# A four-block transformer kernel on one core: the first attention's start reordered, its weight rounding moved to ScalarE and VectorE, and 18 weight-chunk sums moved to VectorE

## The reference, cut to what matters

```python
x = x + attn0(layernorm(x), Wqkv, bqkv, Wo, bo)      # x: 1024 rows of 512
x = x + ffn0(layernorm(x), w1, m1, w2, m2, w3, m3)
x = x + attn1(layernorm(x), ...)                      # 32 heads, top-128 index mask
x = x + lora_ffn(layernorm(x), ...)

def attn0(x, Wqkv, bqkv, Wo, bo):                     # one head of width 128
    q, k, v = split(x @ Wqkv + bqkv)
    return softmax(q @ k.T / sqrt(128)) @ v @ Wo + bo

def ffn0(h, w1, m1, w2, m2, w3, m3):                  # inner width 1792
    W = m + mean(abs(w - m)) * sign(w - m)            # for each of the three pairs
    return (silu(h @ W1.T) * (h @ W3.T)) @ W2.T
```

## Time and profile before

| what | value |
|---|---|
| median of 3 runs | 1438.15 us (1436.08 to 1439.1) |
| time of the profiled execution | 1438.22 us |
| its span, first to last instruction | 1436.4 us |
| mean granted TensorE clock | 0.967 of full speed |
| busy share of the span | PE 92%, PEld 76%, DVE 76%, ACT 58%, POOL 46% |
| matmuls | 7147 |

### The profile page before, as it was taken

How to read it: one execution, slowest core, us unless ns; L and a number is a source line. 1 busy time by engine, 2 the same in 40 slices (tenths; PEclk the granted TensorE clock), 3 DMA queues, 4 the chain that set the end, 5 groups by cost and what they waited for, 6 DMA issues and landing times.

```text
span 1436.4 us, 21267 instructions
## 1 busy us (share of the span) xinstructions
PE 1316.1 (92%) x7147; PEld 1096.2 (76%) x7147; DVE 1091.6 (76%) x2226; ACT 833.0 (58%) x1819; POOL 660.9 (46%) x651
## 2 busy tenths in 40 slices
PE   2968999999899789998769999999999999999998
PEld 1756888888789677775457888888888888888876
DVE  6357334343647599999979998898989889888976
ACT  3783532233246566774557767666776776667761
POOL 5460210010037445645656556555665565566534
PEclk9978999999999899998679999999999999999999
DMA  6560310000212333654720000000000000000021
GB/s 212 159 186 1 117 37 1 1 20 0 69 39 67 107 91 117 227 177 147 276 93 14 1 29 28 28 29 28 19 10 28 28 29 28 29 28 1 16 81 59
DMA packets 83706, 95.52 MB, mean 67 GB/s; under 512 B 11792, under 2 KB 59280, under 8 KB 83088
## 3 DMA queue, kind: packets, MB, share of 16 engines
q1 hardware_dynamic: 83600, 94.17, 20.9%
HBM read 75.27 MB, written 18.87 MB: 66 GB/s over the span
## 4 chain that ended last, share of the span: by engine, by line
PE 68%; DVE 17%; ACT 5%; issue 3%; DMA 2%; SPq 1%; POOL 1%; ACTq 0%; DVEq 0%
PE ps L350 16%; PE ps L352 15%; PE ps L351 15%; PE ps L1877 9%; PE ps L1897 3%; PE ps L1896 3%; DVE acc L1398 3%; DVE top L1409 2%; DVE xn_l L1471 1%; DVE rop L1421 1%; DVE acc L1412 1%; DVE rop L1419 1%; DVE pm L1451 1%; DMA iwq_raw<-in_L_attn_idx_wq_w 1%; DVE rop L1420 1%
## 5 line engine op out<-in xcount | busy, mean ns | idle before, releaser
L753 POOL TENSOR_SCALAR pm<-pm,smx 128x128 f32<-128x128 f32 (+1 forms) x255 | 189.4, 751 | 207.7 <-DVE smx L1458 207.7
L1055 ACT ACTIVATE pm<-pm,smx 128x128 f32<-128x128 f32 (+7 forms) x256 | 197.3, 772 | 35.3 <-DVE smx L1451 34.4
L1451 DVE CUSTOM_DVE_ANT_0 pm<-ps,mbias 128x128 f32<-128x128 f32 (+7 forms) x256 | 191.5, 752 | 27.4 <-PE ps L1877 13.1
L1877 PE MATMUL ps<-ident,pm 128*128 128x128 f32 x1152 | 175.0, 276 | 7.3 <-DVE pTa_l L1471 2.0
L1061 ACT ACTIVATE xn_h<-ps 128x512 fp32r<-128x512 f32 (+3 forms) x256 | 128.6, 513 | 84.1 <-PE ps L1877 81.3
L1471 DVE TENSOR_TENSOR xn_l<-ps,xn_h 128x512 fp32r<-128x512 f32 (+3 forms) x256 | 144.5, 587 | 24.8 <-ACT xn_h L1061 23.8
L350 PE MATMUL ps<-latT_l,qc_h 128*128 128x512 f32 (+3 forms) x384 | 143.3, 373 | 16.7 <-DVE smx L1451 8.7
L1877 PEld LDWEIGHTS ps<-ident,pm 128*128 128x128 f32 x1152 | 132.3, 141 | 33.9 <-issue 11.3
L352 PE MATMUL ps<-latT_h,qc_h 128*128 128x512 f32 (+3 forms) x384 | 134.1, 349 | 0.0
L351 PE MATMUL ps<-latT_h,qc_l 128*128 128x512 f32 (+3 forms) x384 | 133.6, 348 | 0.0
L1398 DVE SCALAR_TENSOR_TENSOR acc<-ps,iw,acc 128x768 f32<-128x768 f32 (+4 forms) x105 | 87.2, 877 | 25.1 <-ACT ps L941 24.6
(11 more groups left out here) (294 smaller groups left out, 3717.8 us busy)
## 6 DMA issues: line engine op xcount, KB each, us to landing
iwq_raw<-in_L_attn_idx_wq_w SPq DMA_DIRECT2D x48, 256.0 KB, 3.5
base<-in_L_ffn_mean_w SPq DMA_DIRECT2D x28, 256.0 KB, 3.1
wring<-in_L_ffn_w SPq DMA_DIRECT2D x21, 256.0 KB, 3.8
ow_raw<-in_L_attn_o_w SPq DMA_DIRECT2D x8, 512.0 KB, 3.9
xn_t<-in_L_attn_o_w SPq DMA_DIRECT2D x8, 512.0 KB, 4.2
wuvo<-pr_even SPq DMA_DIRECT2D x8, 512.0 KB, 5.1
wuvo<-pr_hl SPq DMA_DIRECT2D x8, 512.0 KB, 4.7
wuvo_h<-wuvo SPq DMA_DIRECT2D x16, 256.0 KB, 2.6
```

Of the source, the lines that this page charges most:

```text
L753: pool.tensor_scalar(pm[:, i % 4, 0:w], pm[:, i % 4, 0:w], smx[:, 32 + i:33 + i], 0.0, ALU.mult, ALU.add).then_inc(hd_p, 1)
L1055: act.activation(pm[:, i % 4, 0:w], pm[:, i % 4, 0:w], ACT.Exp, bias=smx[:, i:i + 1], scale=-1.0, accum_out=smx[:, 16 + i:17 + i]).then_in ...
L1451: dve.tensor_tensor_reduce(out=pm[:, i % 4, 0:w], in0=two_banks(2 * (i % 2), w), in1=mbias[:, TRI[t]:TRI[t + 1]], scale=1.0, scalar=3.0 * BIG,
L1877: done = pe.transpose(ps[:, t_bank(p, i), tile(k)], pm[:, tq % 4, tile(4 * c + k)], ident[:])
```

## The change

- Each score row of tile 4 starts at column 192 of the pair of banks, so that it is a matmul of 320 columns in either bank (`row_parts`, `row_block`). The number of matmuls is the same.
- Wqkv is rounded by one ACT instruction and its remainder taken by two DVE instructions (`wqkv_h`, `wqkv_l`), in the first half of the norm; POOL no longer does it. ACT waits for the four loads on `ld_a` ahead of its first `norm_hi`.
- PE makes q of the first four tiles before it transposes tile 4, and a quarter of k of the first four tiles after each of the tiles 4 to 7. Then a value tile, then q and k of the other four. The transposes of this norm use banks 4 and 5.
- Of 18 chunks (kind G) ACT does the sign alone, with no drain, and DVE takes the sum of absolute values from the ring slot. The slot's next load waits for both (`wt_sum`). The others (kind C) stay as they were.
- The bias row is added tile by tile ahead of chunks 16, 18, 20, 22 and 28 (tiles 4 to 7). The first load of w2 waits for all eight.
- The next norm's first `half_norm` and ACT's square root table stand ahead of T7 (N0). The matmul that adds the sums stands behind T7 (M0) and waits for the sums of both engines.

```diff
-ATT_PE = items("S0 S1 V0 V1 V2 V3 Z0 S2 V4 V5 V6 V7 T0 S3 T1 S4 T2 S5 T3 S6 O0 T4 S7 Y0 Y1 T5 Y2 T6 Y3 T7 O1 "
+ATT_PE = items("V1 S0 S1 V2 V3 S2 Z0 V4 V5 V6 V7 T0 S3 T1 S4 T2 S5 T3 S6 O0 T4 S7 Y0 Y1 T5 Y2 T6 Y3 T7 M0 O1 "
                "Y4 Y5 Y6 Y7")
-ATT_ACT = items("C1 S0 S1 C2 V0 C1 S2 C2 V1 T0 C1 T1 S3 C1 T2 S4 C1 T3 S5 C2 S6 C2 O0 T4 C1 S7 C1 T5 C2 T6 C2 T7 O1")
-ATT_DVE = items("S0 S1 V0 B0 S2 V1 T0 S3 T1 S4 T2 S5 T3 S6 O0 T4 S7 Y0 Y1 T5 Y2 T6 Y3 T7 O1 Y4 Y5 Y6 Y7")
-FIRST_CHUNKS = {3: 4, 7: 2}
-ADD_AT = {16: 0, 20: 4}
+ATT_ACT = items("G1 S0 G1 S1 G2 V0 G2 S2 G2 V1 T0 G1 T1 S3 C1 G1 T2 S4 C1 G1 T3 S5 C1 G1 S6 C1 G1 O0 T4 G1 S7 C1 T5 G2 "
+                "T6 N0 T7 O1")
+ATT_DVE = items("S0 S1 A2 V0 A2 S2 B0 A2 V1 A2 T0 S3 A1 T1 S4 A1 T2 S5 A1 T3 S6 A1 O0 A1 T4 S7 A1 Y0 Y1 T5 Y2 A2 T6 Y3 "
+                "N0 T7 O1 Y4 Y5 Y6 Y7")
+FIRST_CHUNKS = "CCCGGCC"
+ADD_AT = {16: (0,), 18: (1,), 20: (2,), 22: (3,), 28: (4, 5, 6, 7)}
...
+ROW_AT = {4: 192}
...
+        def row_parts(b, t):
+            w, at = (t + 1) * P, ROW_AT.get(t, 0)
+            cut = min(512, at + w)
+            parts = [(slice(0, cut - at), ps[:, b, at:cut])]
+            if at + w > 512:
+                parts.append((slice(cut - at, w), ps[:, b + 1, 0:at + w - 512]))
+            return parts
...
                 if last is not None:
                     sp.wait_ge(wt_abs, last + 1)
+                    if last in SUM_APART:
+                        sp.wait_ge(wt_sum, SUM_APART.index(last) + 1)
...
+                if CHUNK_KIND[chunk] == "G":
+                    act.activation(sgn[m][:, s * width:(s + 1) * width], slot, ACT.Sign).then_inc(wt_abs, 1)
+                else:
...
+            first_sqrt(0)
+            act.wait_ge(ld_a, 64)
+            act.activation(wqkv_h[:], raw[:], COPY).then_inc(at_wh, 1)
+            for t in range(4):
+                norm_hi(0, t)
+            weight_chunk()
+            weight_chunk()
+            first_sqrt(1)
+            weight_chunk()
+            for t in range(4, NT):
+                norm_hi(0, t)
+                if t < 6:
                     weight_chunk()
+            first_evict(0)
+            first_evict(1)
+            weight_chunk()
+            first_evict(2)
+            weight_chunk()
+            first_evict(3)
...
+            def first_weights(half):
+                k = slice(2 * half, 2 * half + 2)
+                dve.wait_ge(at_wh, 1)
+                dve.tensor_tensor(wqkv_l[:, k, :], raw[:, k, :], f(wqkv_h[:, k, :]), ALU.subtract).then_inc(at_w, 1)
...
+            def chunk_sum():
+                chunk = apart.pop(0)
+                dve.wait_ge(wt_d, chunk + 1)
+                dve.tensor_reduce(absum[:, chunk:chunk + 1], ring(chunk), AXX, ALU.add, apply_absolute_value=True)\
+                    .then_inc(wt_sum, 1)
...
+            first_roots(0)
+            norm_scale(0, 0)
+            norm_scale(0, 1)
+            first_weights(0)
+            norm_lo(0, 0)
+            norm_scale(0, 2)
+            norm_lo(0, 1)
+            norm_scale(0, 3)
+            first_weights(1)
+            norm_lo(0, 2)
+            dve.wait_ge(ld_x[1], 64)
+            first_stats(4)
+            norm_lo(0, 3)
+            for t in range(5, NT):
+                first_stats(t)
+            first_roots(1)
+            norm_scale(0, 4)
+            for t in range(5, NT):
+                norm_scale(0, t)
+                norm_lo(0, t - 1)
+            norm_lo(0, NT - 1)
+            first_lo(0)
+            first_lo(1)
+            chunk_sum()
+            chunk_sum()
+            first_lo(2)
+            first_lo(3)
...
+            for t in range(4):
+                norm_tile(0, t)
+            pe.wait_ge(ln_lo, 4)
+            pe.wait_ge(at_w, 2)
+            first_product(0, range(NK))
+            for t in range(4, NT):
+                norm_tile(0, t)
+                first_product(1, (t - 4,))
+            value_tile(0)
+            pe.wait_ge(ln_lo, NT)
+            first_product(2, range(NK))
+            first_product(3, range(NK))
...
-                if kind == "T" and i == 7:
+                if kind == "M":
                     pe.wait_ge(wt_abs, 2 * NI)
+                    pe.wait_ge(wt_sum, len(SUM_APART))
...
-                        for b in range(1 if t < 4 else 2):
-                            c = slice(512 * b, min(w, 512 * b + 512))
-                            done = mm3(pe, ps[:, 2 * (i % 2) + b, 0:c.stop - c.start], qc_h[p % 2][:, h, tile(t)],
-                                       qc_l[p % 2][:, h, tile(t)], latT_h[:, 2, c], latT_l[:, 1, c], True, True)
+                        for c, dst in row_parts(2 * (i % 2), t):
+                            done = mm3(pe, dst, qc_h[p % 2][:, h, tile(t)], qc_l[p % 2][:, h, tile(t)],
+                                       latT_h[:, 2, c], latT_l[:, 1, c], True, True)
```

More of the change, by code:

```diff
@@ L582, in _, with output_weights @@
             pool.drain().then_inc(consts, 1)
-            def first_weights():
+            def output_weights():
                 pool.wait_ge(ld_a, 64)
[L586 to L593, removed]
                 pool.tensor_copy(wo_h[:], attn_raw[:, NK * 3 * D0:])
@@ L600, in output_weights, with bias_rows @@
                 pool.tensor_tensor(bv_l[:], bv_f[:], f(bv_h[:]), ALU.subtract).then_inc(at_bv, 1)
-            def bias_rows(first):
+            def bias_rows(tiles):
                 pool.wait_ge(at_zb, 1)
-                for t in range(first, first + 4):
-                    pool.tensor_tensor(xt(t), xt(t), bo_bc[:], ALU.add)
-                pool.drain().then_inc(at_b, 1)
+                for t in tiles:
+                    pool.tensor_tensor(xt(t), xt(t), bo_bc[:], ALU.add).then_inc(at_b, 1)
             for chunk in range(WCHUNKS):
@@ L610, in _ @@
                 slot = ring(chunk)
-                if chunk == 4:
-                    first_weights()
-                elif chunk == 7:
+                if chunk == 9:
                     output_weights()
@@ L806, in weight_chunk, with first_sqrt, first_evict @@
                 act.wait_ge(wt_d, chunk + 1)
[L807 to L812, removed]
+                if CHUNK_KIND[chunk] == "G":
+                    act.activation(sgn[m][:, s * width:(s + 1) * width], slot, ACT.Sign).then_inc(wt_abs, 1)
+                else:
+                    act.activation(sgn[m][:, s * width:(s + 1) * width], slot, ACT.Sign)
+                    act.drain()
+                    act.activation(slot, slot, ACT.Abs, accum_out=absum[:, chunk:chunk + 1])
+                    act.drain().then_inc(wt_abs, 1)
+            def first_sqrt(half):
+                c = slice(4 * half, 4 * half + 4)
                 act.wait_ge(at_rv, half + 1)
-                c = slice(4 * half, 4 * half + 4)
                 act.activation(rs_sqrt[:, c], rs_var[:, c], ACT.Sqrt).then_inc(at_rs, 1)
[L816 to L821, removed]
+            def first_evict(u):
+                m, n = u % 2, u // 2
                 act.wait_ge(at_proj, u + 1)
@@ L1143, in half_norm, with first_stats, first_roots @@
                 rsqrt(k, n, first)
-            def first_norm(half):
+            def first_stats(t):
+                dve.bn_stats(stats[:, 6 * t:6 * t + 6], xt(t))
+            def first_roots(half):
                 c = slice(4 * half, 4 * half + 4)
-                dve.wait_ge(ld_x[half], 64)
-                for t in range(4 * half, 4 * half + 4):
-                    dve.bn_stats(stats[:, 6 * t:6 * t + 6], xt(t))
                 dve.drain()
@@ L1209, in _ @@
                     continue
+                if kind == "A":
+                    for _ in range(i):
+                        chunk_sum()
+                    continue
+                if kind == "N":
+                    half_norm(1, 0)
+                    continue
                 if kind == "B":
```

68 lines of the change are left out of this document (30 added, 38 removed).

## The result

The changed kernel takes 1431.79 us (median of 7 executions, 1429.23 to 1433.69) where the kernel before takes 1436.71 us (7 executions beside it, 1436.08 to 1439.1): a ratio of 0.9961 with an interval of 0.9952 to 0.9971, so it is faster by 4.2 to 6.9 us. The profiled execution took 1430.37 us. The forecast was 1428.9 us, from 1419 to 1435.5: the side and the range hold, the gain was forecast at 9.3 us and is 5.6 by the ratio and 7.9 between the two profiled executions.

What follows compares the result with a forecast made beforehand. Engines wait for each other before the first scores, ACT paces the stretch to O1, DVE the indexer, mostly PE the heads. 1438.2 - 6.6 (at O1) - 2.2 (heads) - 0.5 (indexer) = 1428.9 us; range 1419 to 1435.5.

Steps and rivals of the forecast that it cites:

- Up to the first scores: From the start to the first score matmul: scores at 45.3 us, 6.5 us earlier; bounds 2 and 9.5 us.
- From the first scores to O1: Stretch from first scores to product O1: 55.9 us against 56.0, so 0 gained; 4 us better to 5 us worse.
- the slots' late return: After the first scores, ring slots come back late: third exponential 21.4 us after the scores, against 20.55 before.
- what was saved on ACT is spent waiting: From first scores to O1: ACT has 10.9 us less work, but exponentials wait behind signs of late chunks.
- DVE's full stretch: From O0's remainder at 83.9 us to O1 at 101.2 us: DVE has 17.3 us of work without gaps.
- N0 gives no more: The next norm's root ahead of T7 gains nothing further, as work after T7 lay under O1 before.
- 4 us better if slots come back sooner: Bound on the stretch from first scores to O1, forecast at 0 gained: 4 us gained with earlier slots.
- Tile 4: Score rows 0.14 us shorter; one of two pays in 16 head periods, 2.2 us; 0.5 us more in the indexer.
- ACT's relief shows: Rival, 0.2: few DVE-POOL meetings, slots in time; scores 8.5 us earlier, 4 us gained after: 1423.0 us.
- The sums are held up by POOL: Rival, 0.06: POOL delays DVE's sums by 0.6 us each, 4.8 us in all: 1433.7 us.
- Little is left: Rival, 0.1: the start gains only 2 us and tile 4 nothing to 2.7 us: 1433.5 to 1436 us.
- The slots' turn decides: Rival, 0.1: slot turns over 10.8 us cost more than all gains; at 12 us, O1 at 117.8, time 1445.5 us.

Runs made afterwards that it cites:

- own_load_signal: The changed kernel with a semaphore of its own for Wqkv's load, so its rounding does not wait for three later loads: 1427.66 us, 0.9931 of the kernel before.
- rows_undone: The changed kernel with tile 4's score rows back at column 0: 1433.08 us, 0.9975 of the kernel before.
- root_late: The changed kernel with the next norm's first mean and root (N0) back behind T7, into O1: 1429.75 us, 0.9954 of the kernel before.
- all_full: The changed kernel with all 28 chunks' signs and sums on ACT and no sum on DVE: 1432.3 us, 0.9961 of the kernel before.
- sums_early: The changed kernel with DVE's first chunk sums placed earlier in its order, so slots come back earlier: 1425.1 us, 0.9917 of the kernel before.
- rows_only: The kernel before with only tile 4's score rows moved to column 192: 1434.81 us, 0.9986 of the kernel before.
- combined: The changed kernel with N0 behind T7, the early sums and Wqkv's own semaphore together: 1420.44 us, 0.9882 of the kernel before.
- combined_full: The changed kernel with N0 behind T7, early slots and Wqkv's own semaphore, but all chunks in full on ACT: 1425.84 us, 0.9909 of the kernel before.

## Why the prediction was right or wrong

**Up to the first scores: right in its mechanism, 1.7 us too careful.** I gave 45.3 us, it is 43.60. Wqkv was rounded at 15.0 us and not at 16.2, mostly because the last load landed at 13.5 and not at 14.6. That is 1.2 us of it. DVE then took 10.4 us to the end of its statistics (25.3 us) for my 11.4, and roots and tiles 4 to 7 took 9.6 for my 9.0. The rest held: a remainder beside POOL took 1.98 and 2.02 us (I gave 0.9 and one POOL instruction of 1.28 for each half), a four-element step 1.10 (I gave 0.6 for the meeting), q and k of the other half 36.22 to 41.88 us, 5.7 for my 5.6, and the handing over 1.7 for my 1.7 (41.88 to 43.60). That ACT's wait for all four loads delays the half was right too: taking it away brought 3.8 us.

**From the first scores to O1: the sum came out 3.4 us too low.** I gave 55.9 us; it is 59.3. In the sum's own order: 1.7 us up to the third exponential, 0.5 from there to O0's remainder, 1.1 from there to O1.

- The term for the slots' late return was too small. The exponential that I put at 66.7 us starts at 66.72, but that is chance: the scores came 1.7 us sooner than I had them, so it stands 23.1 us behind them and not 21.4. It does follow the scores. own_load_signal has them 3.8 us earlier and the exponential 4.4 (62.35), and in the four kernels with this order (changed, rows_undone, root_late, own_load_signal) it stands 22.1 to 23.1 us behind them, since the slot that is released at 48.03 us is released behind the maxima of the first two score rows. So "what was saved on ACT is spent waiting" was right in kind and 0.7 to 1.7 us short. One part of it was in no term: the late chain leaves PE idle for 5.28 us, and T1's transposition then runs at the lower clock, 0.8 us longer. From the exponential on, O0's remainder came at 84.44 for my 83.9.
- DVE's full stretch lasted 18.4 us, 84.44 to 102.86, for my 17.3. N0 is 2.6 of it and not 2.1: a step on few elements lasted 0.67 us (at 99.32, ending at 99.99, when POOL's subtraction of 98.84 to 99.97 was over; the same step took 0.17 in sums_early) and DVE waited 0.3 us for ACT's root. A wait of 1.0 us for T5's rounding (ahead of 92.03 us) lay in it as well, which I had not given.
- "N0 gives no more" was too mild. root_late shows that it costs 2.8 us behind O0's remainder (2.1 to 3.2 by the whole stretch), and that the FFN starts no later without it. I had counted its time in DVE's full stretch without drawing the conclusion that it belongs behind T7.

**ACT's relief.** The sums themselves behave as forecast (0.68 us each, 0.60 apart, for my 0.61 to 0.65), and all_full agrees that they bring little. sums_early contradicts the reading that a slot's turn itself had to be that slow: with six of the 18 sums a few places earlier on DVE the stretch takes 52.9 us, 3.1 less than before the change. That is within the bound of "4 us better if slots come back sooner", but 1.5 of the way from 59.3 to it is the clock in O0; without that it is 1.6 less than before the change.

**Tile 4: right in the total and in which row pays, too high for the row.** 2.2 us were forecast in the heads, 2.12 measured by the two rows, 1.8 in rows_only, and nothing in rows_undone. The steps are 0.146 us apart (five of them in 0.73 us, 932.20 to 932.93), what I took from the 512-column row. But the row's saving of 0.14 was wrong. It set six such steps (0.88) against the 1.02 us of a row whose first step was slow; the row at 954.22 has that slow first step too (0.20) and takes 0.93. Rows of one kind differ by 0.09 to 0.10. That S12's saving is kept and S4's lost was right (experiment 1), and 16 times 0.09 would be 1.4 us. The period is 0.13 us shorter all the same: 0.03 more go elsewhere in it, which no run explains, and so the total of 2.2 was partly luck. The page "TensorE: Matmul & The Clock Gate" of the Trainium skill (section "Back-to-back issue gap") has a formula for a single matmul's gap, by which the step would be 0.136 us, an estimate; here the measurement decides, and it is 0.146. In the indexer the 0.5 us is there while tile 4 is worked on: from 502 to 549 us the changed kernel gains 0.7 us on rows_undone, and rows_only gains 0.7 on before over the same rows. In the sum it cannot be seen: from the first FFN to the heads the changed kernel lost 1.0 us against before (5.4 us ahead, then 4.5). DVE is busy 19.97 of 20 us there, as before.

**The rivals.** *ACT's relief shows* (1423.0 us) fell for the changed kernel, though its start, 8.5 us earlier, was nearer than mine; with early sums the time comes near it (1425.1 us), though two remainders still meet POOL there. *The sums are held up by POOL* fell: the sum at 48.63 lies in POOL's 48.18 to 50.73 us and takes 0.68 us, what it takes elsewhere. The page "SBUF — State Buffer" of the Trainium skill (section "Who interferes with whom") says that `tensor_reduce` never contends and that an instruction with two SBUF inputs does. The rows agree with both: this one, and the 0.96 and 2.02 us of own_load_signal. *Little is left* fell at the start and with tile 4. *The slots' turn decides* fell on its slow side: O1 is not later than before. Its mechanism, though, is what put the third exponential 23.1 us behind the scores, 20.6 before.

The whole: 5.0 us at O1 for my 6.6, 2.1 in the heads for 2.2, and nothing for my 0.5 in the indexer make 7.1 us. The profiled pair shows 7.8: 5.4 at the first FFN, 1.0 lost from there to the heads, 2.1 in the heads and 1.2 by the clock at the very end. The ratio over all executions is 5.6, with an interval that reaches 6.9. So the forecast gain of 9.3 was too high by the 1.6 us at O1 and the 0.5 in the indexer, and the rest of the difference lies in what executions of one kernel differ by; no run here divides it further.

## What to carry to other kernels

When work is taken off an engine that waits for a ring of buffers, look first at which instruction hands a buffer back and what stands ahead of it in its queue: releases that stood behind the row maxima cost some 5 us here, and the moved work, worth 6.4 us with early releases, was worth 1.6 to 2.7 without them. Work that is moved ahead of the last step of a full engine is paid in full, and one semaphore shared by a load that is needed now and three that are needed later costs the distance between them. When work is done earlier, look also at what was pushed behind it: two chunks left the part before the scores for the part behind them. When two rows are compared for a saving, take rows of one kind, with the same slow or quick first step.

## What the runs showed of the hardware that was not expected

- DVE's remainder of 768 columns took 0.96 us alone and 1.98 to 2.02 us beside a POOL subtraction, over twice as long, and a four-element step up to 1.10 us in place of 0.16. A pair of scalings of 512 columns, with one tensor as input, took 1.99 us beside POOL (28.50 us in the changed kernel) and 1.00 without it (11.35 us). A row sum with one SBUF input took 0.68 us in both cases, and a remainder that reads PSUM 0.68 to 0.69.
- A part of the program that no edit touched met different granted clocks: 0.68 and 0.74 as the mean of 100 us at the indexer's end, in combined and combined_full. The fall of the clock in O0 was absent in sums_early with no more work on PE ahead of it. The last 38 us of the program had a mean of 0.96 in some kernels and 1.00 in others, worth 1.2 us. This moves a profiled execution by one to several us, as much as some of the edits here.
